# Windowed attention with group norms on one core: five edits to order and waits, and six statistics taken earlier on a semaphore of their own

## What is computed

```python
x = x + attention(gn(x))      # gn: 32 groups of 6 channels, mean and variance over the image
x = x + blur(gn(x))           # shift by whole pixels per channel, then a 5 x 5 Gauss filter

def attention(v):             # windows of 7 x 7 pixels, 12 heads of 16 channels
    q, k, v = w_qkv @ v       # 1 x 1 convolution
    p = softmax(q @ k.T * 16 ** -0.5 + bias)
    return w_proj @ (p @ v) + b_proj
```

## Time and profile before

| | us |
| --- | --- |
| median of 3 runs | 6614.67 |
| lowest and highest | 6597.92, 6614.69 |
| the profiled execution | 6615.9 |
| its span, first to last instruction | 6614.1 |
| mean granted clock of TensorE | 0.881 of full speed |
| PE, PEld busy | 85%, 70% |
| DVE, ACT, POOL busy | 65%, 58%, 60% |

### The profile page before, as it was taken

One profiled execution on the slowest core, in us unless ns is written; L12 is line 12 of the kernel. 1 busy time (PEld: TensorE's weight loads), 2 busy tenths in 40 slices (PEclk: granted clock), 3 DMA queues, 4 the chain that ended last, 5 costly groups with the idle time before them and its releaser, 6 DMA issues. The chain is left out here.

```text
span 6614.1 us, 256680 instructions
## 1 busy us (share of the span) xinstructions
PE 5638.0 (85%) x97860; PEld 4650.4 (70%) x97860; DVE 4323.0 (65%) x9677; ACT 3831.3 (58%) x8451; POOL 3947.8 (60%) x4452
## 2 busy tenths in 40 slices
PE   5888888888888888888888888888888888888886
PEld 4777767776777777677767677767777676777775
DVE  4666666766666666667666666666676666666664
ACT  2655555655556565556555565655565556666553
POOL 1466556665556665556665566655566555666565
PEclk9888888988889898889888888888898888998887
DMA  3555665555665556665555655566655556556554
GB/s 80 110 123 122 125 129 121 114 124 121 127 127 116 122 125 126 128 124 111 126 122 119 129 114 119 123 124 128 126 113 125 118 125 131 123 113 126 123 114 76
DMA packets 1371371, 792.20 MB, mean 120 GB/s; under 512 B 1184840, under 2 KB 1234312, under 8 KB 1365768
## 3 DMA queue, kind: packets, MB, share of 16 engines
q1 hardware_dynamic: 1369992, 773.90, 56.0%
HBM read 156.97 MB, written 154.14 MB: 47 GB/s over the span
## 5 line engine op out<-in xcount | busy, mean ns | idle before, releaser
L1188 POOL TENSOR_TENSOR o<-osb,o 128x192 f16<-128x192 f32 x1024 | 590.9, 577 | 1784.1 <-ACT o L830 1755.5
L1182 POOL TENSOR_TENSOR probl<-prob,probh 98x588 f16<-98x588 f32 x1024 | 1340.5, 1309 | 396.7 <-DVE probh L1029 297.9
L628 PE MATMUL pO<-vv,probh 98*49 98x34 f16 x24576 | 1020.8, 225 | 268.4 <-issue 247.7
L628 PEld LDWEIGHTS pO<-vv,probh 98*49 98x49 f16 x24576 | 870.9, 123 | 462.8 <-issue 418.8
L613 PE MATMUL pT<-qst,kst 96*98 96x49 f16 x12288 | 1045.4, 205 | 30.4 <-issue 30.3
L608 PE MATMUL pT<-mov,biasT 128*98 128x98 f16 x6144 | 1014.3, 233 | 51.3 <-ACT om L838 38.2
L613 PEld LDWEIGHTS pT<-qst,kst 96*98 96x98 f16 x12288 | 981.3, 136 | 69.9 <-issue 33.3
L628 PE MATMUL pO<-vv,probl 98*49 98x34 f16 x12288 | 989.7, 228 | 0.0
L608 PEld LDWEIGHTS pT<-mov,biasT 128*98 128x98 f16 x6144 | 842.4, 137 | 147.1 <-issue 71.7
L822 ACT ACTIVATE mov<-pT 12x98 f16<-12x98 f32 x1024 | 247.2, 241 | 1199.5 <-PE pT L597 1196.6
L1014 DVE TENSOR_REDUCE mx<-pS 128x12 f32<-128x588 f32 x1024 | 779.3, 761 | 155.2 <-issue 137.1
(11 more groups left out here) (184 smaller groups left out, 16621.1 us busy)
## 6 DMA issues: line engine op xcount, KB each, us to landing
kst<-kh SPq DMA_DIRECT2D x1536, 98.0 KB, 2.2
qst<-qh SPq DMA_DIRECT2D x1536, 49.0 KB, 2.3
qst<-mix SPq DMA_DIRECT2D x768, 98.0 KB, 2.8
kst<-mix SPq DMA_DIRECT2D x768, 98.0 KB, 2.6
vv<-cv SPq DMA_DIRECT2D x1024, 73.5 KB
out<-xr SPq DMA_DIRECT2D x256, 294.0 KB
xr<-x_scratch SPq DMA_DIRECT2D x64, 882.0 KB
x_scratch<-xm SPq DMA_DIRECT2D x128, 392.0 KB, 3.9
```

The costliest lines, as they stand in the source:

```text
L628: mm = pe.matmul(pO[64 * win:64 * win + NT, OW * hp:OW * hp + OW], b[0:98, p % 2, PW * hp + NT * win:PW * hp + NT * win + NT], vv[:, g % 2 ...
L1182: pool.tensor_tensor(probl[0:98, p % 2, :], prob[0:98, p % 2, :], probh[0:98, p % 2, :], ALU.subtract).then_inc(S["pl_p"], 1)
L1188: pool.tensor_tensor(o16[:, p % 2, C:2 * C], osb[:, p % 2, :], o16[:, p % 2, 0:C], ALU.subtract).then_inc(S["ol_p"], 1)
```

## The change

The diff has these parts. (1) The loops get `hint_back_edge=True`. (2) SP no longer waits for `y_out` in `store_x1`; the wait stands in step 1 ahead of the read-back, and rows 0 to 41 are read in three pieces in steps 1, 2 and 3 (so `xr_in` counts 128). (3) SP does `spread_v` ahead of `stack` within a step. (4) PE's `shifted` does its six L608 matmuls first, then the twelve L613 ones. (5) The group sums go to `pQ` at the end of PE's steps 12 and 13, without the waits for `max_d`; `add_eps` comes in step 14, POOL's power in step 15. (6) The first load has a semaphore `x_in0` of its own, and of the 12 statistics three each are taken in steps 6, 7, 10 and 11.

```diff
-        PER = {"x_in": 64, "x1_out": 128, "xr_in": 64, "y_out": 8 * 16, "stack_q": 192 * NCH,
+        PER = {"x_in0": 16, "x_in": 48, "x1_out": 128, "xr_in": 128, "y_out": 8 * 16, "stack_q": 192 * NCH,
...
-                with eng.Fori(1, images - 1) as i:
+                with nc.Fori(1, images - 1, engines=bass.OrderedEngineSet([eng.engine]), hint_back_edge=True) as i:
...
-                if k == EARLY // 2 - 1 and due("y_out", i, 0):
-
-                    sp.wait_ge(S["y_out"], nth("y_out", i, 0))
...
+                    v = before(v_step, p, prev, att, nxt) if p % PPR == 2 else None
+                    if v:
+                        spread_v(i + v[0], v[1] // 2)
                     qk = before(qk_step, p, prev, att, nxt)
                     if qk and qk[2] % 2:
                         stack(i + qk[0], qk[1], qk[2] // 2)
-                    v = before(v_step, p, prev, att, nxt) if p % PPR == 2 else None
-                    if v:
-                        spread_v(i + v[0], v[1] // 2)
...
-                    if p == 1 and prev:
-
-                        sp.wait_ge(S["x1_out"], nth("x1_out", i - 1, EARLY * 16))
-                        read_x1(0, EARLY * WS)
+                    if 1 <= p < 4 and prev:
+
+                        if p == 1:
+                            sp.wait_ge(S["x1_out"], nth("x1_out", i - 1, EARLY * 16))
+                            if due("y_out", i - 1, 0):
+                                sp.wait_ge(S["y_out"], nth("y_out", i - 1, 0))
+                        read_x1(2 * WS * (p - 1), 2 * WS * p)
...
-                        sp.dma_start(xm[:, par(i + 1), t], xi[0:CM, t]).then_inc(S["x_in"], 16)
+                        sp.dma_start(xm[:, par(i + 1), t], xi[0:CM, t]).then_inc(S["x_in0" if p == 2 else "x_in"], 16)
...
+                for hp in range(NHP):
+                    bank, at = hp // 3, PW * (hp % 3)
                     for win in (0, 1):
...
-                    if nxt and p in (12, 14):
-
-                        if att:
-                            pe.wait_ge(S["max_d"], nth("max_d", i, p + 1))
-                        pe.wait_ge(S["gn1_dve"], nth("gn1_dve", i + 1, 2 if p == 12 else 6))
-                        group_sum(1, pS[:, 0, 384:386], gmv[0][:, :, 0] if p == 12 else gv[0]).then_inc(S["gn1_pe"], 1)
-                    if nxt and p in (13, 15):
-
-                        pe.wait_ge(S["gn1_dve"], nth("gn1_dve", i + 1, 3 if p == 13 else 7))
...
+                    if nxt and p == 14:
+                        pe.wait_ge(S["gn1_dve"], nth("gn1_dve", i + 1, 7))
...
+                    if nxt and p in (12, 13):
+
+                        if p == 12 and due("qk_dve", i, 12):
+                            pe.wait_ge(S["qk_dve"], nth("qk_dve", i, 12))
+                        pe.wait_ge(S["gn1_dve"], nth("gn1_dve", i + 1, 2 if p == 12 else 6))
+                        group_sum(1, pQ, gmv[0][:, :, 0] if p == 12 else gv[0]).then_inc(S["gn1_pe"], 1)
...
-                        center(0, i + 1, pS[:, 0, 384:386])
-                    if nxt and p == 15:
-                        add_eps(0, i + 1, pS[:, 0, 384:386])
+                        center(0, i + 1, pQ)
+                    if nxt and p == 14:
+                        add_eps(0, i + 1, pQ)
...
-                    if nxt and 10 <= p < 12:
+                    if nxt and p in (6, 7, 10, 11):
+                        if p == 6:
+                            dve.wait_ge(S["x_in0"], nth("x_in0", i + 1, 16))
                         if p == 10:
-                            dve.wait_ge(S["x_in"], nth("x_in", i + 1, 64))
-                        for r in range(6 * (p - 10), 6 * (p - 10) + 6):
+                            dve.wait_ge(S["x_in"], nth("x_in", i + 1, 48))
+                        first = {6: 0, 7: 3, 10: 6, 11: 9}[p]
+                        for r in range(first, first + 3):
...
-                    if nxt and p == 16:
+                    if nxt and p == 15:
...
-                            pool.wait_ge(S["xr_in"], nth("xr_in", i - 1, 64))
+                            pool.wait_ge(S["xr_in"], nth("xr_in", i - 1, 128))
```

More of the change, by code:

```diff
@@ L223, in build @@
             "const_in", "setup", "setup_act", "setup_pe",
-            "x_in", "x1_out", "xr_in", "y_out", "stack_q", "stack_k", "stack_t", "vst0", "vst1",
+            "x_in0", "x_in", "x1_out", "xr_in", "y_out", "stack_q", "stack_k", "stack_t", "vst0", "vst1",
             "gn1_bn", "gn2_bn", "gn1_dve", "gn1_pe", "gn1_pool", "gn2_dve", "gn2_pe", "gn2_pool",
```

## The result

The changed kernel is slower by 1.6%: 6714.1 us, median of 4 runs (6709.94 to 6718.37), against 6614.68 (4 runs) of the kernel before on the same chip, a ratio of 1.0157 with a 95% interval of 1.0139 to 1.0174. The forecast was 6325 us in a range of 6190 to 6490. The profiled span is 6714.3 us at a granted clock of 0.868 (0.881 before).

The account below looks back on a forecast made before the run. The prediction took SP's chain, not PE, to bound the first half of a pass. Its terms, -5.6 + 2.0 + 0.8 - 5.7 - 1.2, gave -9.7 us a pass, -291 us for 30 images: 6325 us from 6615.9, range 6190 to 6490.

Parts of the forecast that it names:

- the pieces: Read-back in steps 1 to 3: some 4.85 us of DMA each; step 7's scores start 5.6 us earlier.
- the group sums: Steps 12 to 14: the wait ahead of scores and its cold stretch go, 16.9 us for 22.64, -5.7 a pass.
- the statistics: Three fewer in steps 10 and 11 shorten the wait for DVE's maximum in step 11: -1.2 us a pass.
- the hold: SP held issuing piece 2, the next image's load and piece 3: 12.7 us, bounds 2.5 and 20.
- the hint: Loop back edge: about 0.5 us stays of 4.2 to 4.5; PE gains 3.7 there and 1.8 in step 0.
- The `y_out` wait: SP's 3.86 us wait goes, nothing is waited in step 1; `qst` starts at 3111.0 instead of 3114.85.
- The swap: `spread_v` first: step 6's wait goes, step 7 idles some 10 us, +2.0 for low clock; step 31 +0.8.
- the matmul order: New order of 18 matmuls in `shifted`: nothing, bounds -0.1 and +0.1 us a step.
- The hint brings nothing: Rival, back edge: still 4.2 us idle, -4.4 us a pass, 6484 us; chance 0.17.
- SP isn't held: Rival, read pieces: they fit the queue, `mix` lands 5.3 us earlier, -15 a pass, 6166 us; chance 0.12.
- The clock: Rival, after step 7's idle: PE stays at 1.2 GHz; six low steps make the pass 11 us longer, 6950 us; chance 0.06.
- Everything cancels: Rival: no hint effect and pieces as slow as step 5's read, about 0 a pass, 6610 us; chance 0.04.

Follow-up runs that it names:

- one read: The changed kernel with rows 0 to 41 read back in one piece in step 1 again: 6460.95 us, 0.9784 of the kernel before.
- The experiment by channel: The changed kernel with its three pieces cut as 42 rows by 32 of 96 channels each: 6496.86 us, 0.9836 of the kernel before.
- the one in step 1: The kernel before with its read cut into three 14-row pieces, all in step 1: 6797.39 us (two of 21 rows: 6720.08), beside 6603.38.

## Why the prediction was wrong

By mean passes, the sum of -9.7 us turned into +3.2. Three of its terms account for the 12.9: the pieces +8.2, the group sums +5.7, and the statistics -1.0. Of what the forecast named as signs, half came true. SP's wait for the outputs and the gap of step 6 are gone, no wait of PE ends with the first load, and the wait for the copies is as large over the run as said. But the edge still shows 1.40 us ahead of PE, and steps 12 to 14 are not near 17.

1. **The price of the pieces (part 2) is the step that failed.** It took "some 4.85 us" for a piece, a third of the read of 42 rows. A piece of 14 rows takes some 7 us, and the trace of before had that read in step 5, 32 times (6.97 us). The prediction used it only as an upper bound of the hold and for a rival with a chance of 0.04, and not as the price. With the rows of step 5, the hold would have been 4.3 us longer (2 x 7.0 for 2 x 4.85) and the four `vv` 4.15 us (8.15 for 4.0): an estimate of 8.4 us more, against the 8.2 that one read shows. With that term alone put right, the sum is about -1.3 a pass.

   The times can be laid side by side if they are counted from SP's `vv` of step 30. The scores of step 7 stood at 53.9 us in the forecast, at 59.5 before, and are at 62.6 after (3143.40 to 3205.99). Of the 8.7 us missed, 3.6 are the first piece and `vv` behind it (9.6 us from the end of q to the start of k, for 6.0), 2.0 the hold and the `mix` copies (22.5 for 20.5), 0.9 the issue of q and k, 1.4 the later start of q, where SP was held 2.73 us by `x_scratch<-xm`, and 0.7 the landing. The stated bound (20) was for the hold alone; the same slow transfer acts on `vv` too, and no bound was set there. The experiment by channel shows the shape as the cause, and the one in step 1 that the place isn't.
2. **With one read that part of the sum holds.** Steps 31 to 7 forecast -2.8 us (-5.6 + 2.0 + 0.8) and take 59.86 with one read against 62.55 before: -2.7. After has +4.9. Within that, though, PE gained only 1.7 in step 31 and 0.4 in steps 0 to 4, not the 3.7 and 1.8 that the forecast gave the hint, so part of the agreement is luck: an error in the hint was made up elsewhere. PE came later to step 7, and its wait there came out at 11.2 us a pass although the copies were late as well: the 10 us and the 250 to 350 us forecast for that wait were met (349.0) for a wrong reason. A symptom that depends on two times doesn't test either.
3. **The group sums (part 5)** were put at -5.7 and brought nothing: 22.60 for 22.48 us. The `gmv` wait is gone as forecast, but PE's mean clock in steps 12 to 14 is 0.77 as before. The sum took for granted that the cold stretch was that wait's, and that nothing else came late in the same step. The rows of before show what did, POOL's `o` for `turn_out`:

```profile
3191.24 0.59 PE L524 MATMUL pS<-gmv,cst 128*128 128x1 f32 x2 [2.23 <-DVE gmv L1047]
3191.52 0.55 POOL L1188 TENSOR_TENSOR o<-osb,o 128x192 f16<-128x192 f32 x1
```

While PE sat behind the aggregates and did the sums, `o` became ready; in the mean it was done only 1.32 us ahead of PE's `turn_out` of step 12, and PE waited for it 0.05 us a pass in these three steps. With the aggregates' wait of 1.54 us gone (mean of step 12) and the sums moved behind, PE waits 1.82 us for `o` instead. PE's idle time in the three steps is 3.29 us a pass after, for 2.92 before. In the pass of after POOL has next to no break ahead of that `o`:

```profile
3232.37 0.93 POOL L1169 TENSOR_TENSOR xnl<-xnf,xnh 128x392 f16<-128x392 f32 x1 [0.16 <-POOL xcf L1229]
3233.63 0.97 POOL L1181 TENSOR_TENSOR xm<-xm,pjt 128x392 f32 x1 [0.33 <-POOL xnl L1169]
3234.68 0.65 POOL L1192 TENSOR_TENSOR o<-osb,o 128x192 f16<-128x192 f32 x1
```

POOL's `o` follows at once behind its work for the blur and the norm, and PE waits 1.55 us for it. One wait took the place of another, and the clock behind it stays low. In the mean step 12 went from 8.87 to 9.64 us, step 13 from 5.06 to 6.86, and step 14 from 8.56 to 6.10: what step 14 gained, the two ahead of it lost, which is also where the sums' matmuls went. Over all the kernels here, with the parts mixed in whatever way, the three steps take 22.1 to 23.1 us. DVE's aggregates now wait for PE's sums in `pQ`, 108.5 us over the run and 3.56 in this pass, where the forecast had up to 1 us; no wait of PE ends with it.

```profile
3241.15 0.16 DVE L1054 COPY gmean<-pQ 128x2 f32<-128x2 f32 x1 [3.56 <-PE pQ L526]
```

That PE's wait for `o` replaced the one for `gmv` is shown. That POOL's work is what makes `o` late is argued, not shown: the run with less of it did not shorten the steps. What sets their 22 to 23 us stays open.
4. **The statistics** were right in sign and low in size, 2.2 for 1.2 us, since the wait for `mov` wasn't counted. The wait for the first load, said to bring nothing on DVE, is 165.6 us over the run, 8.20 in the pass shown, and costs nothing all the same: PE isn't let in until 3205.99.

```profile
3195.04 1.50 DVE L1141 BATCH_NORM_STATS2 gst<-xm 128x6 f32 x3 [8.20 <-DMA xm<-in_x]
```

The load lands 43.5 us behind the start of step 0 (3151.54); the forecast had 35 (3145 behind 3110.2).
5. **The `y_out` wait** cost SP 3.86 us in the pass of before, and is worth 0.7 alone: `x_scratch<-xm`, which now goes first behind the outputs, holds SP for 2.73 us where it took 1.40; the rest of what came back wasn't traced. **The swap** costs 0.5 us a pass for a forecast of 0.8, which is within noise of nothing, and **the matmul order** costs nothing, as forecast.
6. **The rivals.** The hint brings nothing: wrong, though PE keeps more than half of its gap. The Trainium skill (Runtime: NRT & Kernel Launch, Instruction fetch mechanics) calls prefetch purely sequential; the edge of DVE fell from 4.53 to 0.55 us in the pass shown and so speaks against the word for a hinted edge, while PE's 2.9 does not settle it. SP isn't held: wrong, and in the opposite direction. The clock: wrong; behind 15.87 us of idle the 6.18 us of step 7 that are left run at 0.53, and the next step is at the full 1.00, 2.4 GHz, as it is in all of the 28 passes:

```profile
3212.17:3216.70 4.53, 4.53 (x86) 3.39 (x84) 3.24 (x10) 3.39 (x8) 2.55 (x3) 1.00 0.99 67
```

Everything cancels was nearest, with pieces as slow as in step 5; it had 0.04, and it asked for a hint without effect as well. The 0.06 for slower had come from the clock alone. No rival had slow pieces beside a hint that works. The term with the sign of the forecast in it was priced by proportion, although the row of its shape was at hand.

## What to carry to other kernels

A transfer cut in pieces is not priced by its bytes. Look first for a transfer of the new shape in the trace that you have: here it was one read further on, and its time and that of the copies queued behind it would have given the loss to within some 0.5 us a pass. If there is none, take a bound that moves every transfer queued behind a piece too. Where a cut is needed, try the dimension that leaves the number of rows written by each DMA as it was; here that kept 217 of 253 us.

A wait removed from a step counts only up to what comes ready next in the same step. Look at how long before its use each other input of the step was done. Here `o` was done 1.32 us ahead, and three steps stayed at 22 to 23 us through a removed wait, an earlier one and less work beside it.

## What the runs showed of the hardware

- The same packets (224 bytes, 8064 of them in all) took 15.8 us in one read of 42 rows, 18.7 in two of 21 and 23.3 in three of 14, back to back in one queue; and 4.9 us against 7.2 for a third of them by channel and by row. The two reads of 21 rows had 8.0 packets in flight at once, those of 42 and of 14 rows 16 to 17. While the first piece of after moved, the DMA share was 1.11 at 95 GB/s, against 1.14 at 134 in the one read the earlier trace rows: the DMA engines were as occupied and moved less.

```profile
3163.00:3169.60 6.60, 6.60 (x109) 5.06 (x108) 5.07 (x10) 6.42 (x13) 3.15 (x4) 1.00 1.11 95
```

- A queue holds the engine that issues: SP stood 17.02 us on six DMAs of 14 rows, 5.98 on two of 42, and 7.71 to 10.90 on four short `vv` copies behind such a read, where they take 3.36 with none ahead.
- A hinted back edge cuts the branch's cost from 4 to 5 us to under 0.6 on DVE, ACT and POOL. PE keeps 2.9 of 4.75 us, and SP shows 0.2 to 0.3 us with and without the hint.
- Behind a gap of 15.87 us PE worked 6.18 us at a clock of 0.53, and the step after that ran at 1.00.
- Regrouping weight loads of 128 and 96 rows changed nothing that could be measured (1.0005, 0.9984 to 1.0027).
